# Mixture layers of a two-layer decoder: the scatters are issued choice by choice between weight roundings, and the chosen matrix is written by an addition

## The reference, cut to what matters

```
# layer 0: 16 routed experts of inner width 352 (gate and up), 2 shared experts, 6 choices per token
scores = sigmoid(h @ gate_weight.T); by_choice = scores + bias
keep the 2 groups (of 4) whose two best by_choice add up to most; top-6 experts in them
w = scores[top6] / (sum + 1e-20) * 2.5
out = shared(h) + sum_j w_j * expert_j(h),  expert(h) = (silu(h @ gate.T) * (h @ up.T)) @ down.T
# layer 1: 8 routed experts, 1 shared, 2 choices, softmax probabilities, expert(h) = silu(h @ w1) @ w2
```

## Time and profile before

| | us |
|---|---|
| median of three timed executions | 1998.75 |
| span of the profiled execution (its own time around the span isn't given) | 2063.0 |
| TensorE busy in the span | 1842.6 |
| GpSimd busy in the span | 1001.5 |
| VectorE busy in the span | 1111.7 |

### The profile page before, as it was taken

One profiled execution on the slowest core, in us unless ns is written; L12 is line 12 of the kernel. 1 busy time (PEld: TensorE's weight loads), 2 busy tenths in 40 slices (PEclk: granted clock), 3 DMA queues, 4 the chain that ended last, 5 costly groups with the idle time before them and its releaser, 6 DMA issues.

```text
span 2063.0 us, 30652 instructions
## 1 busy us (share of the span) xinstructions
PE 1842.6 (89%) x10235; PEld 1599.9 (78%) x10241; DVE 1111.7 (54%) x2750; ACT 788.0 (38%) x2029; POOL 1001.5 (49%) x964
## 2 busy tenths in 40 slices
PE   6999899753999999799769999999999999988796
PEld 4888777543899898699657888888887888876685
DVE  5666875451333333233656666666666667455244
ACT  3766542200222222122146556656564433213231
POOL 3434431584383759891736645456453003007584
PEclk8999999976999999999989999999999999889898
DMA  3556320353353445532433333233321210003465
GB/s 105 166 159 191 135 104 1 114 195 121 114 204 118 156 166 184 190 123 71 139 97 98 98 87 90 63 94 98 82 69 43 65 46 21 1 29 115 147 222 180
DMA packets 102693, 232.32 MB, mean 113 GB/s; under 512 B 18816, under 2 KB 19072, under 8 KB 99472
## 3 DMA queue, kind: packets, MB, share of 16 engines
q1 hardware_dynamic: 82224, 144.11, 23.1%
q0 software_dynamic: 19744, 85.47, 12.1%
q10 hardware_dynamic: 576, 0.79, 0.1%
HBM read 126.23 MB, written 57.93 MB: 89 GB/s over the span
## 4 chain that ended last, share of the span: by engine, by line
PE 70%; DVE 6%; POOL 6%; another core or an unknown queue 4%; DMA 3%; ACT 3%; issue 3%; SPq 3%; ACTq 0%; DVEq 0%; POOLq 0%
PE bank L149 57%; PE bank L957 3%; PE bank L941 2%; PE bank L2049 2%; PE bank L2040 2%; DMA a_g<-a_f 2%; SPq L620 2%; SPq L605 1%; POOL a_g L651 1%; POOL f_UL L161 1%; DMA a_QL<-a_g 1%; PE bank L327 1%; POOL a_E L657 1%; PE bank L938 1%
## 5 line engine op out<-in xcount | busy, mean ns | idle before, releaser
L657 POOL TENSOR_SCALAR a_E<-a_E,a_inv 128x128 f32<-128x128 f32 (+3 forms) x384 | 219.8, 590 | 222.4 <-DVE a_inv L792 222.4
L149 PE MATMUL bank<-f_UH,f_XH 128*128 x596 | 201.4, 338 | 22.1 <-POOL f_UL L161 16.4
L690 ACT ACTIVATE a_E<-a_E,a_top 128x512 f32<-128x512 f32 (+3 forms) x384 | 211.2, 567 | 7.8 <-DVE a_top L786 7.7
L149 PE MATMUL bank<-f_UL,f_XH 128*128 x596 | 193.6, 325 | 0.0
L149 PE MATMUL bank<-f_UH,f_XL 128*128 x596 | 193.4, 325 | 0.0
L682 ACT ACTIVATE a_PHL<-bank 128x512 fp32r<-128x512 f32 (+1 forms) x288 | 130.9, 528 | 132.8 <-PE bank L957 132.8
L149 PE MATMUL bank<-a_PHL,a_VH 128*128 128x512 f32 (+3 forms) x768 | 180.8, 324 | 0.3 <-DVE a_QL L161 0.3
L786 DVE CUSTOM_DVE_ANT_0 a_E<-a_causal,bank 128x512 f32<-128x512 bf16 (+3 forms) x384 | 163.8, 482 | 30.6 <-PE bank L941 19.0
L1708 DVE TENSOR_TENSOR f_gate<-bank,f_gate 128x352 f32<-128x352 f32 x79 | 41.4, 524 | 251.0 <-PE bank L149 209.7
L1651 ACT ACTIVATE f_HH<-bank 128x256 fp32r<-128x256 f32 x220 | 60.0, 325 | 301.9 <-PE bank L2040 223.3
L149 PE MATMUL bank<-f_DH,f_HH 128*128 (+1 forms) x330 | 141.0, 427 | 32.1 <-DVE f_HL L161 26.3
(11 more groups left out here) (397 smaller groups left out, 5054.6 us busy)
## 6 DMA issues: line engine op xcount, KB each, us to landing
f_uraw<-f_up POOLq DMA_DIRECT2D x18, 1408.0 KB, 6.3
f_xb<-table SPq DMA_DIRECT2D x86, 256.0 KB
table<-f_ob SPq DMA_DIRECT2D x86, 256.0 KB
table<-a_zeros SPq DMA_DIRECT2D x31, 512.0 KB, 4.4
f_draw<-f_down POOLq DMA_DIRECT2D x27, 512.0 KB
a_g<-a_f SPq DMA_DIRECT2D x160, 64.0 KB, 2.0
a_raw<-a_qkv SPq DMA_DIRECT2D x36, 256.0 KB, 3.4
f_uraw<-f_up POOLq DMA_DIRECT2D x9, 704.0 KB, 4.5
```

The costliest lines, as they stand in the source:

```text
L149: m = pe.matmul(out, a, b, start=first and i == 0 and j == 0, stop=last and i == n - 1 and j == 2, skip_group_check=not check)
L657: e.tensor_scalar(self.E[sl][:, a], self.E[sl][:, a], self.inv[:, sl, i:i + 1], 0.0, ALU.mult, ALU.add).then_inc(*self.s_nrm.up(N, m - 1, i))
L690: x = e.activation(E, E, ACT.Exp, scale=-1.0, bias=self.top[:, sl, i:i + 1], accum_out=self.total[:, sl, i:i + 1])
```

## The change

Three edits. First, GpSimd's order: the scatters of one choice become a function `_send(j)`, and they are issued between weight roundings. Layer 0 goes: up 1, down 1, up 2, send 0, down 2, send 1, wait for step 7, send 2, up 3, send 3, down 3, send 4, send 5. Layer 1 goes: up 1, down 1, up 2, send 0, down 2, send 1, wait for step 7, up 3, down 3. Second, VectorE's last addition in `_largest` goes; the two copies become additions of `chosen` and `both` (returned as `level`), so the generator has one piece less. Third, every register that is loaded from SBUF for a wait goes through a register operation that takes the maximum with 1 (63 and 23 on TensorE, 25 on GpSimd in the two layers).

```diff
-        for w in (1, 2):
-            self._up(w)
-            self._down(w)
+        self._up(1)
+        self._down(1)
+        self._up(2)
         for j in range(self.top):
-            e.wait_ge(*self.s_idx.after(N, j))
+            self._send(j)
             if j == 0:
-                e.wait_ge(*self.k.s_cleared.after())
-            for i in range(NT):
-                e.indirect_dma_start(out=self.k.table[0:self.NR * P, :],
-                                     out_offset=bass.IndirectOffsetOnAxis(ap=self.idx[:, j, i:i + 1], axis=0),
-                                     in_=self.rows[i], in_offset=None).then_inc(*self.s_sent[j].up(N))
-        e.wait_ge(*self.s_out.after(N, NT - 1))
-        self._up(3)
-        self._down(3)
+                self._down(2)
+            if j == 1:
+                e.wait_ge(*self.s_out.after(N, NT - 1))
+            if j == min(2, self.top - 1):
+                self._up(3)
+            if j == min(3, self.top - 1):
+                self._down(3)
...
+    def _load_bounded(self, e, loaded, to, of):
+        e.reg_load(loaded, of)
+        for reg, x in zip(to, loaded):
+            e.reg_alu(reg, x, 1, ALU.max)
...
-        e.tensor_tensor(above, above, both, ALU.add).then_inc(*d.up())
-        yield
+        return both
...
-        e.tensor_copy(self.turns(self.chosen[:, 0:NT, :]), self.in_turn(C)).then_inc(*self.s_chosen.up(N))
+        e.tensor_tensor(self.turns(self.chosen[:, 0:NT, :]), self.in_turn(chosen), self.in_turn(level),
+                        ALU.add).then_inc(*self.s_chosen.up(N))
         yield
-        e.tensor_copy(self.turns(mine), self.in_turn(C)).then_inc(*d.up())
+        e.tensor_tensor(self.turns(mine), self.in_turn(chosen), self.in_turn(level), ALU.add).then_inc(*d.up())
```

More of the change, by code:

```diff
@@ L110, in constants @@
         self.table = self.nc.dram_tensor("table", [tiles * P, D], F32).ap()
+        self.pe_loaded = [self.pe.alloc_register(f"loaded{i}") for i in range(8)]
         self.pe_registers = [[self.pe.alloc_register(f"tile{g}_{i}") for i in range(8)] for g in range(2)]
+        self.pool_loaded = [self.pool.alloc_register(f"expert_loaded{i}") for i in range(4)]
         self.pool_registers = [self.pool.alloc_register(f"expert{i}") for i in range(5)]
@@ L1522, in pool @@
                 regs = self.k.pool_registers[0:n]
-                e.reg_load(regs, self.ends[0:1, w - 4:w - 4 + n])
+                self._load_bounded(e, self.k.pool_loaded[0:n], regs, self.ends[0:1, w - 4:w - 4 + n])
             e.wait_ge(self.s_out.sem, regs[(w - 4) % 4])
@@ L1545, in pool, with _send @@
             self._gather(j, i)
+    def _send(self, j):
+        e, N = self.k.pool, self.name
+        e.wait_ge(*self.s_idx.after(N, j))
+        if j == 0:
+            e.wait_ge(*self.k.s_cleared.after())
+        for i in range(NT):
+            e.indirect_dma_start(out=self.k.table[0:self.NR * P, :],
+                                 out_offset=bass.IndirectOffsetOnAxis(ap=self.idx[:, j, i:i + 1], axis=0),
+                                 in_=self.rows[i], in_offset=None).then_inc(*self.s_sent[j].up(N))
     def _gather_early(self, j):
@@ L1555, in _gather_early @@
         reg = self.k.pool_registers[4]
-        e.reg_load([reg], self.ends[0:1, self.R + j:self.R + j + 1])
+        self._load_bounded(e, self.k.pool_loaded[0:1], [reg], self.ends[0:1, self.R + j:self.R + j + 1])
         e.wait_ge(self.s_ev.sem, reg)
@@ L1824, in _largest @@
         yield
-        e.wait_ge(*d.now())
-        e.tensor_tensor(above, above, both, ALU.add).then_inc(*d.up())
-        yield
+        return both
     def _route(self):
@@ L1876, in _route @@
             yield
-            yield from self._largest(gt.rearrange("p (t g) s -> p t (g s)", g=G), chosen)
+            level = yield from self._largest(gt.rearrange("p (t g) s -> p t (g s)", g=G), chosen)
         else:
@@ L1896, in _route @@
             yield
-            yield from self._largest(sc, chosen)
-        C, self.taken["early"] = chosen, kept
+            level = yield from self._largest(sc, chosen)
+        self.taken["early"] = kept
         mine, share = late("mine", [NT, R]), late("share", [NT, R])
         e.wait_ge(*d.now())
-        e.tensor_copy(self.turns(self.chosen[:, 0:NT, :]), self.in_turn(C)).then_inc(*self.s_chosen.up(N))
+        e.tensor_tensor(self.turns(self.chosen[:, 0:NT, :]), self.in_turn(chosen), self.in_turn(level),
+                        ALU.add).then_inc(*self.s_chosen.up(N))
         yield
-        e.tensor_copy(self.turns(mine), self.in_turn(C)).then_inc(*d.up())
+        e.tensor_tensor(self.turns(mine), self.in_turn(chosen), self.in_turn(level), ALU.add).then_inc(*d.up())
         yield
@@ L2102, in _weights_at @@
         if i % 8 == 0:
-            e.reg_load(self.k.pe_registers[i // 8 % 2][0:min(8, self.NR - i)], self.owner[0:1, i:i + min(8, self.NR - i)])
+            m = min(8, self.NR - i)
+            self._load_bounded(e, self.k.pe_loaded[0:m], self.k.pe_registers[i // 8 % 2][0:m], self.owner[0:1, i:i + m])
         reg = self.k.pe_registers[i // 8 % 2][i % 8]
```

## The result

In the first comparison the changed kernel took 2023.86 us (median of 2022.62, 2025.09, 2028.32 and 2021.68) and the kernel before 1998.38 us (four executions, 1996.85 to 1999.92). The ratio is 1.0135, 95% interval 1.0113 to 1.0157: slower by 25.5 us, where 2024.0 was forecast. Later, on two chips, the same two kernels gave the opposite sign: 2033.5 against 2055.1 us (0.9895, 0.9858 to 0.9931) and 2036.4 against 2058.9 us (0.990, 0.9855 to 0.9944); on one more, before took 2063.3 us. The chip of the first comparison isn't on record, so it could be one of these at another time. So there are two results, and what follows has to explain both.

What follows compares the result with a forecast made beforehand. TensorE's gaps bound the kernel, with the profiled stall taken as recording's. Scatter chain +24.8 (routing's 1.3 gain included), clock +0.5, registers +0.2, layer 1 0: 25.5 on 1998.75 gives 2024 us; 8-in-10 range 1984 to 2034.

Steps and rivals of the forecast that it cites:

- The upper bound of +33: Whole kernel: most the change could cost, with the register price, layer 1's 3 us and a slower clock.
- the register price of 8.6: TensorE's 86 register maxima: 0.1 us each, up to 8.6 us if nothing hid them; 0.2 was taken.
- The scatter chain: GpSimd, layer 0: scatters queued behind step 7's wait and w = 3's roundings delay tiles 2 to 5; tile 6 24.8 us later.
- the slowed clock: TensorE behind load waits in layer 0: the slowdown falls into the next wait; 0.5 us added for the last.
- The start: TensorE, layer 0: step 7's transposes at 454.9 in the changed kernel, GpSimd held at its wait until 459.1.
- The routing: VectorE, layer 0: cast of 5.60 us becomes about 0.3, net 0 for TensorE; smaller savings give 1.3 us.
- Registers, layer 1: Two terms: 111 register maxima cost 0.2 us; layer 1's order changes 0, from -2 to +3.
- I take the stall as something that recording causes: Profiled gaps beside scatters, 54.2 us in layer 0 and about 8 in layer 1, are absent from timed runs.
- My chance of 0.70 for "slower": Whole kernel: slower by the scatter chain, chance 0.70, own range 2014 to 2032 us.
- 62 us against 64: Both layers' stall, 62 us, explains the 64 us by which the timed median lies below the profiled span.
- the stall is the chip's own and real: Rival, chance 0.22: the stall beside scatters is in timed runs too; the change gains 34 us, to 1965.
- the sign of being wrong that I had named: Whole kernel: the prediction is wrong if the timed median falls with the profiled span.

Runs made afterwards that it cites:

- the paced kernel: Changed kernel with `_down(2)` ahead of all 48 scatters, five tiny memsets behind each, step 7's wait and w = 3 last: 2055.49 us, 0.9978 of before.

## Why the prediction was right, and where it wasn't

**The number.** 2024 forecast, 2023.86 measured, in the comparison it was made for. The mechanism, four waits of tiles 2 to 5 behind GpSimd's chain, is in the changed kernel's trace line by line. That before has no such waits in the same condition is worked out and not seen, and the last microseconds of the agreement are luck (see the sum below). The upper bound of +33 doesn't follow from its own terms: the register price of 8.6 in place of 0.2 and layer 1's 3 alone bring the 25.5 to 36.9. Nothing hung on it.

**The scatter chain.** Every term of it holds within 0.4 us, on a start that was 3 us off. Release behind step 7: 459.1 forecast, 462.38 measured. Starts of tiles 2 to 5: 473.6, 493.4, 510.5, 520.6 forecast; 476.73, 496.95, 514.09, 524.18 measured, that is +3.1, +3.6, +3.6, +3.6. Waits 2.4, 13.1, 10.4, 3.4 forecast; 2.25, 11.66, 8.02, 0.98 by the profile, since the step behind each wait takes 8.6 to 9.1 us instead of 6.7 at a granted clock of 0.73 to 0.80: the slowed clock falls into the next wait, as forecast. Load 2.8, measured 2.9.

**The start.** Step 7's transposes came at 458.0 and not 454.9, because steps 5 and 6 take 9.5 and 7.8 us instead of 6.26. No signal is late there. VectorE's gate product of step 5 starts only at 443.28, behind seventeen operations on the choices' weights. Of the six of one kind among them, three take 1.71, 1.07 and 0.95 us beside GpSimd's roundings of 436.06 to 441.5, the other three 0.29. In the traces of before and of the paced kernel, where no rounding runs beside them, all six take 0.29. The Trainium skill (SBUF — State Buffer, section "SBUF: two separate sides") gives VectorE operations with two SBUF inputs and GpSimd operations that read SBUF one shared pair of ports, which one of them holds for its whole instruction; the 1.71 beside 0.29 agrees. Step 6 is late for another reason: TensorE was busy throughout, and its granted clock was at half (1.2 GHz) from 443.8 to 447.2, behind the wait of 2.40 us for that gate product. In the paced kernel, where the roundings of w = 2 stand ahead, steps 5 to 7 come at 6.3 us each. I had put the routing at net 0 and missed that `_down(2)` moves beside this tail of it.

**The routing.** Right as far as the cast goes: matrix at 415.44 + 0.38 instead of 422.73, and the next piece that needs TensorE waits 4.79 us for it. Steps 3 and 4 together take 1.7 us less than before, 1.3 forecast. With the old order the new routing measured 0.9996, under late signals. The index of choice 0 came 3.2 us earlier (425.57 for 428.81), 1.4 of it because the whole trace is that much ahead; forecast 1.5.

**Registers, layer 1.** 0.2 forecast, not measurable. In layer 1, step 9's transposes come 8.3 us behind step 8's where before has 6.1, which would be +2 within my -2 to +3; but in the two later traces of the changed kernel it is 7.8 and 6.3. The span of the 31 steps fell from 161.6 to 155.8 us with the late signals gone, so the rest can't be told apart.

**The step that failed: "I take the stall as something that recording causes".** That before's timed runs at 1998 us are free of the stall was right: the stall alone is 54 us. The reason doesn't hold as stated. The changed kernel ran in the first comparison with no late signal in its trace, and in two later ones with them; all its executions there have a span on record 1.35 to 1.48 us below their time, so all were recorded alike, and recording alone doesn't make signals late. And before took 2047 to 2075 us in 52 of 52 executions on three chips, not 1998. So there is a condition that some chips or some hours have and others not, and it decides the sign. My chance of 0.70 for "slower" was thus a bet on which condition the timing would meet, and I didn't see it as one.

What isn't shown is that recording has no part in it. The text ahead of the prediction calls the executions timed without the profiler. But each of the 52 has a span and a granted clock on record as well, so they are no unrecorded runs; for before's four at 1998 us neither is given. No kernel was run both ways in one comparison, and the records that go missing beside the indirect transfers, in this condition alone, would fit a path of records that is overfull there as well as one of the updates themselves. The rule that I cited from the Trainium skill (NOTIFIC — the notification-queue block, section 7.1), that this path pushes back on its producers rather than lose a record inside the block, is neither borne out nor refuted by these runs: signals were late, and records are missing as well, wherever that happened.

**The sum that agreed.** "62 us against 64" was partly luck. 2063.0 less 1997.0 (the median less the 1.4 us around a span) is 66.0. But this gap also holds what the condition costs elsewhere: from step 33 to 78 before takes 329.6 us and the changed kernel of the first comparison 318.1, 11.5 less (3.4 of it the granted clock at steps 34 and 47), and behind layer 1's last gate transposes 23.8 against 21.0. That leaves 51.7 for the scatters of both layers, and I counted 62: by this estimate some 10 us of what I took for stall are there without late signals too. So before was later than my sum had it, and the changed kernel was as well, by 3.6 us at tile 6 (530.9 for 527.3). These two errors offset each other in the difference, which came out at 25.5 as forecast. That before's part is the same kind of tail as in steps 5 and 6 of the changed kernel is argued, not shown: there is no trace of before without late signals.

**The rival "the stall is the chip's own and real"** describes the later comparisons, where the median fell together with the span, the sign of being wrong that I had named. It gave -34 us. Measured: -21.5 and -22.5. Its terms by the traces: tile 6 from 553.4 to 531 (-22 where -26 was forecast; the start again), layer 1 -5 where -8 was forecast (161.6 to 156.5), and the price of late signals elsewhere stays for both. It took the stall to begin 13 us into the row; the first late update is that of a product that ended at 439.84, 9 us into it, and bursts of eight already show waits of 6 us.

**Open.** What sets the condition: chip, time or neighbours, and whether it takes recording to show. No kernel of mine switched it. It isn't recording alone, and under late signals the old order alone, with or without the new registers and routing, has the full stall.

## What to carry to other kernels

Check that a trace and the timed median are of the same condition before you subtract them: a gap of span and median may be a passing condition, and then the forecast needs one number for each condition with a chance on each. A trace shows which it is of: count its records of landings against the transfers issued. On GpSimd, break up a long row of indirect transfers, but with as little as does it, and never put a wait or a rounding that nothing needs yet ahead of a transfer that a load in order stands behind. Keep an order's benefit and its cost apart by testing one move at a time; here the same order was 25 us worse and 22 us better.

## What the runs showed of the hardware

While GpSimd issues indirect transfers of 128 rows of 2 KB every 1.27 us, TensorE's semaphore updates can arrive 12 to 53 us late (439.84 to 451.95, 443.86 to 496.78), and those of VectorE and ScalarE that have a record don't. The first late one belongs to a product that ended 9 us into the row. At one transfer in 1.44 us the longest wait for such a signal was 11.8 us, at 1.60 us 7.4, in bursts of eight and sixteen at 1.27 us with longer breaks 6.2, at an even 2.04 us there was none in 97 us. It happens on some chips or at some times only: the same changed kernel ran at 2022 us with no such wait and at 2038 us with them, and the same kernel before at 1998 and at 2063.

Where signals are late, records of updates are missing beside indirect transfers, and only there: 93 of 768 landings of the scatters on record at one in 1.27 us, 322 in the changed kernel, 663 at one in 2.04 us; without late signals 768 of 768. What a late signal is in such a trace, a late update or a late effect of recording, the runs don't tell.

Behind a wait of TensorE of 8.0 to 11.7 us for a load, the step of 6.7 us took 9.1 at a granted clock of 0.73 and 0.74. And the 3.4 us at half the clock around a wait of 2.2 us for a rounding came in some traces and not in others (0.84 against 1.00 in the same step 34), for 1.5 us.
